# A gated delta-rule layer and its ternary feed-forward: one pair's first norm and feed-forward are done in the next pair's turn

## The reference, cut to what matters

```python
q = causal_dwconv_silu(x @ Wq.T, conv_wq)    # 4 taps per channel; k and v alike
beta = sigmoid(x @ Wb.T)
g = -exp(A_log) * softplus(x @ Wa.T + dt_bias)
q = l2norm(q) * DK ** (-0.5); k = l2norm(k)
def step(S, inp):                            # over the 256 tokens
    S = S * exp(gt); v_new = vt - kt @ S
    S = S + bt * outer(kt, v_new)
    return S, qt @ S
o = o * rsqrt(mean(o * o) + eps) * norm_w * silu(x @ Wg.T)
x = layernorm(x + o @ Wo.T)                  # the first norm
x_q = where(x > 0.33, 0.5, where(x < -0.33, -0.5, 0.0))
w = where(W > 0.2, 0.6, where(W < -0.2, -0.6, 0.0)) + rram_variation
x = layernorm(x + x_q @ w.T)                 # the second norm
```

## Time and profile before

| | |
|---|---|
| median of 3 runs | 385.25 us (385.13, 385.25, 390.33) |
| the profiled execution, its own time | 389.6 us |
| its span, first to last instruction | 387.8 us |
| granted clock of TensorE, mean | 0.841 |
| busy: TensorE, VectorE, ScalarE, GpSimd | 254.6, 282.4, 139.6, 9.4 us |
| instructions | 15259 |

### The profile page before, as it was taken

The page is one execution under the profiler, slowest core; times in us unless marked ns, Lnnn a source line. Parts: engine busy times, 40 slices in busy tenths (PEclk is TensorE's granted clock), DMA queues, the critical chain, the costliest instruction groups (busy, mean ns, idle before and its releaser), DMA issues.

```text
span 387.8 us, 15259 instructions
## 1 busy us (share of the span) xinstructions
PE 254.6 (66%) x6994; PEld 185.0 (48%) x6994; DVE 282.4 (73%) x718; ACT 139.6 (36%) x280; POOL 9.4 (2%) x14
## 2 busy tenths in 40 slices
PE   2992649876567948676698576955756647554650
PEld 1491424466544616475566254854543447553430
DVE  0574898865979987578989874979798742219996
ACT  0694515425444242273362613643513103141010
POOL 2000100001000000010000000100000000000000
PEclk9985797959999986889989969799869668995775
DMA  8700000000000010000010100000100001001001
GB/s 240 289 0 0 3 2 0 3 3 5 4 5 2 2 54 0 5 6 4 5 57 0 54 3 3 5 5 3 59 0 1 0 5 57 6 3 56 3 0 54
DMA packets 8016, 9.78 MB, mean 25 GB/s; under 512 B 1808, under 2 KB 7056, under 8 KB 7952
## 3 DMA queue, kind: packets, MB, share of 16 engines
q1 hardware_dynamic: 7024, 8.41, 6.4%
q10 hardware_dynamic: 928, 0.39, 0.4%
HBM read 6.70 MB, written 2.10 MB: 23 GB/s over the span
## 4 chain that ended last, share of the span: by engine, by line
PE 40%; DVE 34%; issue 16%; ACT 7%; DMA 2%; DVEq 0%; SPq 0%; ACTq 0%
PE fr L325 10%; PE pj L338 7%; PE pg L325 5%; PE pc L325 4%; PE fr L507 4%; PE po L325 4%; PE fr L590 2%; DVE t_all L879 2%; DVE t_all L878 2%; DVE r_all L880 2%; ACT x_buf L739 2%; DMA xt<-x_t 2%; DVE o_all L1047 1%; DVE m_o L1041 1%; PE pj L353 1%
## 5 line engine op out<-in xcount | busy, mean ns | idle before, releaser
L900 DVE SCALAR_TENSOR_TENSOR conv_buf<-raw,wconv,conv_buf 128x512 f32<-128x512 f32 x72 | 52.8, 750 | 15.3 <-ACT conv_buf L642 13.6
L338 PE MATMUL pj<-xt,wproj 128*128 128x512 f32 x96 | 49.6, 663 | 13.1 <-DMA xt<-x_t 7.2
L338 PEld LDWEIGHTS pj<-xt,wproj 128*128 128x128 f32 x96 | 19.5, 214 | 36.2 <-issue 26.4
L641 ACT ACTIVATE raw<-pj 128x512 f32<-128x512 f32 x24 | 14.3, 597 | 43.2 <-PE pj L338 43.2
L1031 DVE TENSOR_TENSOR mq<-fr,ad 128x512 f32<-128x512 f32 x12 | 8.3, 691 | 21.3 <-PE fr L325 21.3
L325 PE MATMUL fr<-kga,wu 32*32 32x64 f32 x768 | 14.7, 230 | 10.0 <-issue 9.9
L353 PE MATMUL pj<-xt,wproj 128*128 128x512 f32 x48 | 21.3, 593 | 0.0
L668 ACT ACTIVATE kq<-conv_buf 64x256 f32<-64x256 f32 (+1 forms) x24 | 11.5, 486 | 20.9 <-DVE conv_buf L900 20.8
L325 PEld LDWEIGHTS fr<-kga,wu 32*32 32x32 f32 x768 | 13.2, 116 | 11.1 <-issue 11.1
L325 PE MATMUL pg<-x,p_sb 32*32 32x16 f32 x768 | 10.0, 192 | 11.8 <-issue 11.1
L507 PE MATMUL fr<-wsplit,tok_buf 128*128 128x256 bf16 x72 | 15.1, 404 | 3.3 <-ACT tok_buf L753 3.3
(11 more groups left out here) (171 smaller groups left out, 602.5 us busy)
## 6 DMA issues: line engine op xcount, KB each, us to landing
xt<-x_t SPq DMA_DIRECT2D x1, 1536.0 KB, 9.2
res<-x SPq DMA_DIRECT2D x3, 512.0 KB, 4.1
out<-hid_buf SPq DMA_DIRECT2D x6, 256.0 KB, 2.6
wproj<-w_proj SPq DMA_DIRECT2D x1, 1024.0 KB, 7.9
xt<-x_t SPq DMA_DIRECT2D x1, 512.0 KB, 5.8
kq<-x SPq DMA_DIRECT2D x1, 512.0 KB, 3.9
out<-wu SPq DMA_DIRECT2D x2, 256.0 KB, 2.1
wout<-w_out SPq DMA_DIRECT2D x1, 384.0 KB, 9.7
```

The costliest lines, as they stand in the source:

```text
L338: mm = pe.matmul(pj[:, j % 2, :], wproj[:, t, j * P:(j + 1) * P], xt[:, t, k * TOK:(k + 1) * TOK], start=(t == 0), stop=(t == KT - 1))
L641: act.activation(raw[:, j, :, TAPS - 1:], bank, ACT.Copy)
L900: e = dve.scalar_tensor_tensor(out=conv[:, d, :, :], in0=raw[:, d, :, m:m + T], scalar=wconv[:, j, m:m + 1], in1=conv[:, d, :, :], op0=ALU ...
```

## The change

On each engine the end of the layer of pair k is taken out of turn k and put into turn k+1:

- VectorE: `attention_sum`, `first_norm` of pair k-1 stand before `inverse(k)`, `ternary(k - 1)` behind it; then come the taps and transition sums; `feed_forward_sum(k - 1)` and its moments follow `factors(k + 1)`. The substitution is in one piece, right behind the gating and `chunk_matrices`. The reciprocal root of the second norm is taken along by `head_norm` instead of by `factors`.
- TensorE: the turned ternary values come after the second bank of `solved`, the products after the third and fourth chunk of the state loop (c = 2, 3). `merge(k + 1)` follows the last gate; projection 4 of the pair after next comes between `merge` and `merge_second`, projection 5 behind `merge_second`, where before 4 stood before `merge` and 5 behind it.
- ScalarE: `normalize(k - 1, 0)` between the copies of projections 4 and 5; `ternary_out(k - 1)` after two banks of `solved_out`; the first three SiLUs after the first state; `normalize(k - 1, 1)` behind the four copies of the next projections.
- Memory: the turned values go through bank `pj[:, 0]` instead of `pg`, the products into `pj` instead of `fr`. The SiLU of the values writes in place (`conv`) and into a small `v_last`, so `v_to_tokens` has four transposes for two; `x1_buf` and `xq_t` have places of their own.

The diff, cut to its core (the three functions `turn` are, in this order, those of TensorE, ScalarE and VectorE):

```diff
             def exponents(k):
                 if not first(k):
                     after(pe, gate_done, 0, k, GATE_TILES)
+                    after(pe, ffn_in, 0, k - 1, 2)
...
             def merge_second(k):
-                if not first(k):
-                    after(pe, xqt_done, 0, k, 1)
...
-                if b == 2 and not first(k):
-                    after(pe, ffn_in, 0, k, 2)
...
-            def feed_forward(k):
+            def ternary_turned(k):
                 after(pe, xq_done, 1, k, 1)
+                if last(k + 1):
+                    after(pe, gate_done, GATE_TILES, k + 1, GATE_TILES)
+                else:
+                    after(pe, tile_out, 5, k + 2, CONV_TILES)
...
             def turn(k, front):
                 merge_second(k)
-                for b in range(5):
+                if front:
+                    project(k + 1, 5)
+                solved(k, 0)
+                solved(k, 1)
+                if not first(k):
+                    ternary_turned(k - 1)
+                for b in range(2, 5):
                     solved(k, b)
...
                     heads_out(k, c)
+                    if not first(k) and c in (2, 3):
+                        feed_forward(k - 1, c - 2)
                 if front:
                     exponents(k + 1)
                     for g in range(G3):
                         chunk_products(k + 1, g)
                     if not last(k + 1):
-                        project(k + 2, 0)
-                        project(k + 2, 1)
-                        project(k + 2, 2)
+                        for j in range(4):
+                            project(k + 2, j)
+                    gates(k + 1, 0)
+                    gates(k + 1, 1)
                     project_out(k, 0)
                     project_out(k, 1)
-                    if not last(k + 1):
-                        project(k + 2, 3)
-                    for j in range(GATE_TILES):
-                        gates(k + 1, j)
-                    feed_forward(k)
-                    feed_forward_products(k, 0)
-                    feed_forward_products(k, 1)
+                    gates(k + 1, 2)
+                    merge(k + 1)
                     if not last(k + 1):
                         project(k + 2, 4)
-                    merge(k + 1)
-                    if not last(k + 1):
-                        project(k + 2, 5)
...
-            for j in range(4, CONV_TILES):
-                project(1, j)
             merge(0)
+            project(1, 4)
...
             def turn(k, front):
                 merge_out(k)
                 if front:
+                    tile_out_of_psum(k + 1, 4)
+                if not first(k):
+                    normalize(k - 1, 0)
+                if front:
                     tile_out_of_psum(k + 1, 5)
-                if front:
-                    silu(k + 1, 0)
-                    silu(k + 1, 1)
-                for b in range(5):
+                solved_out(k, 0)
+                solved_out(k, 1)
+                if not first(k):
+                    ternary_out(k - 1)
+                for b in range(2, 5):
                     solved_out(k, b)
-                    if front and b == 1:
-                        silu(k + 1, 2)
                 state_out(k, 0)
                 if front:
-                    silu(k + 1, 3)
-                    square(k + 1)
+                    for j in range(3):
+                        silu(k + 1, j)
                 for c in range(1, NC):
                     if c < NC - 1:
                         state_out(k, c)
                     if c % 2:
                         heads_out(k, c // 2)
...
+                    if not front:
+                        if c % 2:
+                            heads_square(k, c // 2)
+                        continue
+                    if c == 1:
+                        square(k + 1)
+                    if 3 <= c < 6:
+                        silu(k + 1, c)
+                    if c >= 5:
+                        heads_square(k, c - 5)
+                    if c == NC - 1:
+                        heads_square(k, 3)
...
             def turn(k, front):
                 head_eps(k)
+                if first(k):
+                    conv_taps(1, 0)
+                else:
+                    attention_sum(k - 1, 0)
+                    attention_sum(k - 1, 1)
+                    first_norm(k - 1)
+                inverse(k)
+                if not first(k):
+                    ternary(k - 1)
                 if front:
-                    conv_taps(k + 1, 0)
-                inverse(k)
+                    for j in range(first(k), 3):
+                        conv_taps(k + 1, j)
+                for b in range(3):
+                    transition_sum(k, b)
                 if front:
-                    for j in range(1, 4):
+                    kq_to_tokens(k + 1)
+                    for j in range(3, CONV_TILES):
                         conv_taps(k + 1, j)
-                    kq_to_tokens(k + 1)
-                else:
+                    factors(k + 1)
+                if not first(k):
+                    feed_forward_sum(k - 1)
+                    after(dve, ffn_in, 2, k - 1, 2)
+                    moments(hid)
+                if not front:
                     rsqrt(r_n, v_n, t_n)
                     shifts()
-                transition_sum(k, 0)
-                transition_sum(k, 1)
-                transition_sum(k, 2)
-                if not front:
                     return
-                conv_taps(k + 1, 4)
-                conv_taps(k + 1, 5)
-                factors(k + 1, not first(k))
                 scaled_operands(k + 1)
                 v_to_tokens(k + 1)
                 head_norm(k)
                 gated(k)
                 chunk_matrices(k + 1)
-                for j in range(1, 7):
-                    substitute(j)
-                attention_sum(k, 0)
-                attention_sum(k, 1)
-                first_norm(k)
-                for j in range(7, 10):
-                    substitute(j)
-                ternary(k)
-                for j in range(10, HALF - 1):
+                for j in range(1, HALF - 1):
                     substitute(j)
                 inverse_to_rows(k + 1)
-                feed_forward_sum(k)
-                after(dve, ffn_in, 2, k, 2)
-                moments(hid)
```

More of the change, by code:

```diff
@@ L210, in program @@
         s_bank = (pc, po)
+        f_bank = (pj[:, 1, :], pj[:, 0, :])
         o_bank = (pg[:, :], fr[:, 2, :])
@@ L909, in kq_to_tokens @@
                 after(dve, silu_done, 3, k, CONV_TILES)
-                if not first(k):
-                    after(dve, ffn_mm, 0, k - 1, 2)
+                if k > 1:
+                    after(dve, xqt_mm, 0, k - 1, 1)
                 dve.transpose(kq_tok[:, :, :, :, :].rearrange("p g k c d -> p (g k c d)"),
@@ L919, in v_to_tokens @@
                 for h in range(2):
-                    e = dve.transpose(kr[:, :, :, DK + 32 * h:DK + 32 * h + 32].rearrange("p c g v -> p g c v"),
-                                      v_ch[:, :, h, :].rearrange("p g (c t) -> p g c t", c=NC))
+                    cols = slice(DK + 32 * h, DK + 32 * h + 32)
+                    own.counted(dve.transpose(kr[:, :, 0:2, cols].rearrange("p c g v -> p g c v"),
+                                              conv[:, VTILE_LO + h, :, :].rearrange("p g (c t) -> p g c t", c=NC)))
+                    e = dve.transpose(kr[:, :, 2, cols], v_last[:, h, :].rearrange("p (c t) -> p c t", c=NC))
+                    if not h:
+                        own.counted(e)
                 e.then_inc(v_tok_done, 1)
@@ L1097, in first_norm @@
                 moments(hid)
+                if not first(k):
+                    after(dve, out_done, 0, k, 2)
                 rsqrt(r_n, v_n, t_n)
@@ L1267, in _ @@
             dve.wait_ge(beta_in, 24)
-            factors(0, False)
+            factors(0)
             scaled_operands(0)
```

81 lines of the change are left out of this document (33 added, 48 removed).

## The result

The changed kernel takes 370.29 us (median of 4 runs, 368.7 to 371.11) against 387.79 us for the kernel before, run again beside it: a ratio of 0.954 [0.944, 0.964]. The prediction was 366 us, of a median of 385.25 us: a ratio of 0.950. The profiled execution agrees more closely: its span is 368.1 us where the sum of the terms gave 368.6. It agrees partly because two terms were wrong in opposite directions.

A forecast was written before the change was run, and what follows sets the result against it. VectorE was taken as nearly the bound in middle turns, waiting on TensorE round trips. Terms 79.2 + 69.6 + 73.4 + 73.4 + 73.0 gave 368.6 us against 387.8; 19.2 less than the 385.25 median gave 366, forecast 363 to 372, range 360 to 378.

The forecast's parts named there:

- The bound and the direction: VectorE nearly the bound in middle turns, waiting on TensorE round trips; faster (under 377.5 us) had a chance of 0.84.
- Second half: Middle turn, head norm to next release: 34.2 us, including 1.0 us of VectorE stall for the merge; before 48.6.
- My sign that I would be wrong: Merge still stalling VectorE over 3 us, head norm waiting on squares, or middle-turn feed-forward sum waiting for TensorE.
- First half, 39.2: Middle turn, from release (end of the last multiplication in `inverse`) to head norm: 39.2 us, before 31.8.
- First interval, 69.6: First release to second, with nothing deferred yet: 35.4 plus 34.2, 69.6 us instead of 80.9.
- Last interval, 73.0: Last release to end of span, deferred work new in the path: 67.7 becomes 73.0 us, tail starting 32.6 after release.
- transposes 1.05 and both halves 2.5 each: TensorE's feed-forward work in the last turn's state loop; products end 28.2 us after the release if nothing hides them.
- relief: Last turn: inserted products fill TensorE's 1.36 us instruction gap, ending 26.8 us after the release; 27.5 taken.
- B: Merge wholly covered (4 times 1.0 back) and transition sums at 14.5 us or sooner: 360 to 361 us; chance 0.12.
- A: TensorE's section bounds the first half, feed-forward halves about 8.4 us together: 378 us; chance 0.20 with lesser forms.
- C: Slower: VectorE's mid-turn waits for products add up round a ring with TensorE and ScalarE; up to 397 us; chance 0.06.
- The page's rule: Instruction-store refill is mostly hidden, so inserted products hide nothing: last interval 73.7 us; the sum used the trace rows instead.

The follow-up runs named there:

- first_norm_own_turn: Changed kernel with the residual sums and first norm back in the pair's own turn, behind the sixth substitution step: 388.0 us, ratio 0.998 to the kernel before.
- ff_products_twice: Changed kernel with the 24 feed-forward products of each deferred pair done twice into the same banks: 376.7 us, ratio 0.969 to the kernel before.
- ff_products_late: Changed kernel with the deferred feed-forward products behind state-loop chunks c = 5 and 6 instead of 2 and 3: 384.8 us, ratio 0.989 to the kernel before.
- p4_behind_second: Changed kernel with projection 4 moved behind the second round of the merge, next to projection 5: 376.8 us, ratio 0.969 to the kernel before.
- block_edge_at_merge: Changed kernel with projection 4 before the merge, then 102, 51 and 71 small products without use: 380.4 us, ratio 0.980 to the kernel before.
- merge_short_edge_bad: Changed kernel, merges cut to 338 products, projection 4 before them, then 110, 99 and 0 products without use: 372.1 us, ratio 0.964 to the kernel before.
- merge_short_edge_good: Changed kernel, merges cut to 338 products, projection 4 before them, then 40, 99 and 0 products without use: 366.7 us, ratio 0.949 to the kernel before.

## Why the prediction was right or wrong

*The bound and the direction: right.* VectorE's own work stayed, its waits went, and the middle turns are VectorE's with the merge wait. first_norm_own_turn shows which cover did it.

*Second half, "a stall of 0 to 2.5 us, and I take 1.0": this is a term that was mis-sized.* It measured 3.6, 3.7 and 2.7 us; the middle turns' halves took 36.8 and 35.8 instead of 34.2. The cover was right to 0.3 us (6.9 from the merge's first product to the end of VectorE's first piece, for 7.2); the merge's length was not. I had taken its 8.0 to 9.3 us from turns in which the feed-forward products and a projection ran just before it, and the granted clock in it was 1.00. Started after 4.7 to 6.2 us without work, it took 9.5 to 10.6: at 0.50 the first round took 2.75 us for 1.79, and the projection inside it 3.7 or 3.8 for 1.98. In turn 3, which has no projection inside, the second round stopped for instructions, the last time for 2.10 us. My sign that I would be wrong, more than 3 us of stall, came true in two turns.

*First half, 39.2: right to 1.8 us.* It measured 38.6 and 37.4. The transition sums ended 14.95 us after the release in turn 1 (14.9 forecast) and 13.8 in turn 2, which is where the second gained. VectorE came to the feed-forward sum after 29.0 us (29.3 forecast). The four value transposes take 1.84 us for the two's 1.79, so the 0.4 was nearly nothing.

*First interval, 69.6: 70.5,* with a first half of 33.8 for 35.4 and a second of 36.7 for 34.2. The transition sums ended 13.6 us after the release (14.5 forecast). The head norm's squares were never waited for; the longer wait before the first transition sum came as said, 5.0 us.

*Last interval, 73.0: the second mis-sized term, 69.1.* The step "transposes 1.05 and both halves 2.5 each" took a half's time from the earlier trace rows, where the granted clock over the products was 0.54. In the state loop it is 1.00 and a half takes 1.49, the transposes 0.62. The products ended 23.6 us after the release, not 27.5, and the tail began at 28.7, not 32.6. The shorter steps are some 2.5 of these 3.9 us. The rest is relief that I had put too low: the second half began at 321.07, 22.1 us after the release, just where the rows had the fourth chunk end without any inserted products. So, against those rows, the transposes and the first half had cost nothing by then. All that follows the products (sum, moments, root) was right to 0.1 us.

*The sum.* The errors were +0.6, +0.9, +2.0, -0.1 and -3.9 us: 368.1 for 368.6 is partly luck. The subtraction from the median was fair: 385.25 was at the low end of the kernel before, whose later medians were 386 to 389.

*Rivals.* B did not happen, and it was miscounted: it gives back four stalls of 1.0 us, where the sum has three. A is refuted by ff_products_twice, and no head norm waited for its squares. Its 8.4 us for both halves doubled a row of 2.10 us as if that were the full clock; at 1.00 both take 3.0 us, and at 0.54 they took 5.0. C did not happen, but its first step did where it was provoked: in ff_products_late VectorE waits in mid-turn for late products, 3.0 and 3.5 us in the two middle turns. There the price was 1.3 and 1.8 us of interval, under C's one for one; the last interval grew by 6.6 us. And p4_behind_second pays for a copy that stands ahead of a normalisation in ScalarE's order.

*The page's rule.* The forecast held the sentence of the Trainium skill against the gaps. The size of a block in the Trainium skill, "Runtime: NRT & Kernel Launch", section "Instruction fetch mechanics" (256 instructions, refilled in whole blocks), agrees with stops 128 pairs apart. That the refill is mostly hidden doesn't hold here: where the edges lay made 5.3 us between two kernels whose merges have the same work, and 11 us between two others. The kernels of a pair differ in 70 and in 64 products without use.

## What to carry to other kernels

Look for the longest round trip to another engine on the bound engine's chain and put the neighbour pair's independent work there; here, without that one cover, nothing was left of the gain. The cover needs the rest to be deferred with it, since the rest waits for its result. Take the duration of a moved step from a row at the clock of the place that it moves to, and of a round trip from one that starts in the same state. When a burst of several hundred small instructions waits for its input, where the instruction blocks end inside the burst can cost as much as what stands beside it (0 against 3.1 us for one merge here), and every inserted instruction moves all edges behind it.

## What the runs showed of the hardware that was not expected

In its bursts of small products TensorE stopped for instructions 128 pairs of weight load and product apart, and neighbouring stops ended 3.3 to 5.0 us apart (in block_edge_at_merge the merge began at 219.01 and went on at 222.48, 226.81 and 230.26; in merge_short_edge_bad 142.47 and 147.46). 64 more products without use in idle time, 102 for 38 in one turn, made the whole kernel 11 us slower. Keeping the clock up through the idle made 125 small products take 1.22 us and gained nothing measurable in a kernel whose edges had moved too. When a block is asked for is read from the stops only: the pair merge_short_edge_good and merge_short_edge_bad agrees with "on entering the one before", and no record in the trace shows the request itself.
